# Delta rule stage of a two-layer kernel: joint level products, block-sized merges, a second state buffer, a transferred output matrix and new engine orders

## The reference

```python
q, k, v = short_conv(h @ Wq), short_conv(h @ Wk), short_conv(h @ Wv)    # 4 taps, then silu
g = exp(-softplus(h @ Wfa @ Wfb + dt_bias) * exp(A_log))                # per token, head, key
beta = sigmoid(h @ Wb);  q = l2norm(q) * DK ** -0.5;  k = l2norm(k)
def step(S, inp):                        # S: keys x values, one per head
    S = S * gt[..., None]
    pred = einsum('bhk,bhkv->bhv', kt, S)
    delta = (vt - pred) * bt[..., None]
    S = S + kt[..., None] * delta[:, :, None, :]
    o = einsum('bhk,bhkv->bhv', qt, S)
o = o * rsqrt(mean(o * o) + EPS) * norm_w * sigmoid(h @ Wga @ Wgb);  x = x + o @ Wo
```

## Time and profile before

| what | value |
|---|---|
| median of 3 runs | 1812.22 us (1808.32 to 1816.23) |
| the profiled execution's own time | 1804.4 us |
| its span, first to last instruction | 1802.4 us |
| busy in the span: TensorE, VectorE, ScalarE, GpSimd | 1547.0, 1338.2, 1034.1, 41.3 us |
| mean granted clock of TensorE | 0.93 |

### The profile page before, as it was taken

How to read it: one execution, slowest core, us unless ns; L and a number is a source line. 1 busy time by engine, 2 the same in 40 slices (tenths; PEclk the granted TensorE clock), 3 DMA queues, 4 the chain that set the end, 5 groups by cost and what they waited for, 6 DMA issues and landing times. The chain is left out here.

```text
span 1802.4 us, 33031 instructions
## 1 busy us (share of the span) xinstructions
PE 1547.0 (86%) x10840; PEld 1067.9 (59%) x10840; DVE 1338.2 (74%) x3718; ACT 1034.1 (57%) x2716; POOL 41.3 (2%) x49
## 2 busy tenths in 40 slices
PE   6867889786878778999999998999999899888678
PEld 2534555563535246767766766776777677677535
DVE  6649989956722388889889889888898998984121
ACT  6317878876310455866766676586676667643210
POOL 0000000000000000000000000000000000000000
PEclk9989899989889879999999999999999999989589
DMA  2023000001010211011201101111110110100010
GB/s 103 25 75 93 11 10 5 2 1 77 25 52 18 63 29 43 16 52 51 61 12 55 58 12 57 58 38 29 57 55 12 60 54 16 45 28 7 1 52 24
DMA packets 84071, 69.42 MB, mean 39 GB/s; under 512 B 58673, under 2 KB 72625, under 8 KB 82625
## 3 DMA queue, kind: packets, MB, share of 16 engines
q1 hardware_dynamic: 83904, 67.31, 12.3%
HBM read 58.33 MB, written 6.98 MB: 36 GB/s over the span
## 5 line engine op out<-in xcount | busy, mean ns | idle before, releaser
L1524 DVE SCALAR_TENSOR_TENSOR arena<-arena 128x1024 f32<-128x1024 f32 x144 | 184.1, 1279 | 30.6 <-ACT arena L1101 29.8
L789 PE MATMUL bank<-xt,arena 128*128 128x512 f32 x384 | 197.4, 648 | 4.5 <-ACT arena L1093 3.1
L1582 DVE COPY_PREDICATED arena<-arena,bank 128x512 f32<-128x512 int32 x160 | 185.0, 1175 | 0.3 <-issue 0.3
L842 PE MATMUL bank<-arena 128*64 128x64 f32 x3072 | 143.8, 238 | 36.6 <-DVE arena L1604 21.7
L842 PEld LDWEIGHTS bank<-arena 128*64 128x64 f32 x3072 | 117.0, 144 | 84.0 <-issue 54.6
L1602 DVE TENSOR_TENSOR arena<-arena 128x512 f32<-128x512 f32 x224 | 156.4, 698 | 3.3 <-PE bank L842 2.9
L639 PE MATMUL bank<-xt,arena 128*128 128x512 f32 x320 | 143.5, 604 | 5.5 <-DVE arena L1344 3.9
L789 PEld LDWEIGHTS bank<-xt,arena 128*128 128x128 f32 x384 | 73.7, 209 | 74.8 <-issue 71.8
L639 PEld LDWEIGHTS bank<-xt,arena 128*128 128x128 f32 x320 | 60.3, 193 | 89.6 <-issue 83.6
L658 PE MATMUL bank<-arena 128*128 128x256 f32 (+2 forms) x384 | 102.3, 416 | 11.0 <-DVE arena L1344 10.2
L1100 ACT COPY arena<-bank 128x512 f32<-128x512 f32 x96 | 56.5, 589 | 91.7 <-PE bank L789 91.7
(11 more groups left out here) (169 smaller groups left out, 3563.6 us busy)
## 6 DMA issues: line engine op xcount, KB each, us to landing
arena<-zero_scratch SPq DMA_DIRECT2D x29, 512.0 KB, 3.8
arena<-d_w SPq DMA_DIRECT2D x16, 519.0 KB, 6.1
arena<-beta_scratch SPq DMA_DIRECT2D x16, 512.0 KB, 5.4
arena<-f_up SPq DMA_DIRECT2D x2, 1408.0 KB, 6.3
arena<-w_scratch SPq DMA_DIRECT2D x2, 1376.0 KB, 6.1
arena<-f_idx SPq DMA_DIRECT2D x2, 1072.0 KB, 9.7
w_scratch<-arena SPq DMA_DIRECT2D x2, 1072.0 KB, 4.0
arena<-a_wq SPq DMA_DIRECT2D x16, 128.0 KB, 2.7
```

Source lines behind the costliest of these rows:

```text
L789: last = pe.matmul(bank[b][:], DW[:, par, c:c + P], XT[:, k, rhs], start=(k == 0), stop=(k == KC - 1))
L842: last = pe.matmul(to[:, :, p], KL[:, par, r], rhs, start=True, stop=True)
L1524: dve.scalar_tensor_tensor(out=CT[:, x], in0=RAW[:, x, 3 - j:3 - j + S], scalar=DW[:, par, tap:tap + 1], in1=CT[:, x], op0=ALU.mult, op1=A ...
L1582: dve.copy_predicated(out, mask, bank[b][:].rearrange("p (c b s) -> p c b s", c=8, s=s)).then_inc(free[b], 1)
```

## The change

Level products of both groups go into one bank (64 columns per chunk), banks 2 and 3 alternate by level, PE's step is split into `low` and `high` (`top` is level 6). The output matrix's lower half is therefore written at columns 0 to 63 and moved by a transfer (`mb_moved`), and the old place cleared (`mb_cleared`). Masks, XX and PM are 64 columns wide or less. `left` and `right` multiply diagonal blocks of 2s x 2s alone; at level 5 ACT copies instead of DVE. `norm_q` is four matmuls of 256 columns and a VectorE transpose. SS has two buffers, and `predict` and `update` lose their bank 6 matmuls to `out` and `out_end`. PLACE is new on all engines. Cut to its core:

```diff
+    "pe": [
+        (1.169, "piece", 3), (1.27, "piece", 2), (1.343, "piece", 6), (1.452, "piece", 7), (1.608, "piece", 5),
...
+        (2.56, "turn_v", 0), (2.586, "turn_v", 1), (2.6373, "low", 0), (2.6673, "high", 0), (2.6794, "low", 1),
+        (2.7104, "high", 1), (2.7247, "low", 2), (2.7502, "high", 2), (2.8123, "low", 3), (2.8214, "high", 3), (2.86, "norm_q"),
+        (2.9257, "low", 4), (3.0639, "high", 4), (3.123, "gate", 0), (3.2507, "low", 5), (3.285, "gate", 1),
+        (3.3144, "high", 5), (3.4294, "top", 1), (3.4295, "left", 4), (3.4541, "right", 4), (3.4915, "top", 0),
+        (3.5312, "left", 5), (3.5698, "right", 5), (3.6044, "left", 6), (3.6785, "right", 6), (3.699, "keys", 0),
+        (3.728, "solve", 0), (3.774, "update", 0), (3.7741, "out", 0), (3.814, "predict", 1), (3.883, "solve", 1),
+        (3.917, "update", 1), (3.9662, "out_end", 0), (3.991, "predict", 2), (4.0147, "out", 1), (4.025, "solve", 2),
...
+        (4.2582, "out_end", 4), (4.283, "solve", 5), (4.288, "out", 5), (4.295, "update", 5), (4.2955, "out_end", 5),
+        (4.32, "predict", 6), (4.337, "solve", 6), (4.3655, "out", 6), (4.367, "update", 6), (4.4079, "out_end", 6),
+        (4.426, "predict", 7), (4.452, "solve", 7), (4.4868, "out", 7), (4.4971, "out_end", 7), (4.552, "update", 7),
...
+        (5.322, "project", 1), (5.574, "project", 0),
...
+    "act": [
...
+        (3.264, "gate", 0), (3.328, "gate", 1), (3.3405, "level", 5), (3.4512, "left", 4), (3.4871, "top", 1),
...
+    "dve": [
...
+        (3.196, "less", 11), (3.212, "less", 12), (3.213, "less", 13), (3.224, "less", 14), (3.232, "advance", 4, 0),
+        (3.234, "total", 4), (3.252, "advance", 4, 1), (3.3037, "level", 4), (3.312, "total", 5), (3.356, "advance", 5, 0),
...
...
+                    sp.wait_ge(free[2], read(2, m, "low", LEVELS - 3))
+                    sp.wait_ge(free[3], read(3, m, "low", LEVELS - 2))
+                    sp.dma_start(MB[64:P, par, :, 1, 64:P], MB[64:P, par, :, 1, 0:64]).then_inc(mb_moved, 16)
                     sp.wait_ge(inverse_out, 32 * (m + 1))
                     wait(sp, x_zero, 16 * m)
                     wait(sp, y_zero, 16 * (m - 1))
                     for k in range(NB):
-                        ks = slice(BLK * k, BLK * (k + 1))
-                        sp.dma_start(XX[ks, :, ks], blk_x.rearrange("(k c) (i a) -> k i c a", k=NB, i=BLK)[k]).then_inc(x_put, 16)
+                        ks, at = slice(BLK * k, BLK * (k + 1)), BLK * k % 64
+                        sp.dma_start(XX[ks, :, at:at + BLK], blk_x.rearrange("(k c) (i a) -> k i c a", k=NB, i=BLK)[k]).then_inc(x_put, 16)
                         sp.dma_start(YY[ks, par, :, ks], blk_y.rearrange("(k c) (a i) -> k a c i", k=NB, a=BLK)[k]).then_inc(y_put, 16)
+
+                def clear(m, par):
+
+                    sp.wait_ge(mb_moved, 16 * (m + 1))
+                    sp.dma_start(MB[64:P, par, :, 1, 0:64],
+                                 zeros[64:P, 0:NT * 64].rearrange("p (c k) -> p c k", c=NT)).then_inc(mb_cleared, 16)
...
-                for t in range(NT):
-                    last = pe.matmul(bank[0][:, t:t + 1], RAW[:, 0, 4 + t * P:4 + (t + 1) * P], ONES[:, 0:1], start=True, stop=True)
+                q = RAW[:, 0, 4:].rearrange("p (c j i) -> p j c i", j=4, i=32)
+                for j in range(4):
+                    last = pe.matmul(bank[0][32 * j:32 * j + 32, 0:2 * P], ONES[:, 0:32], q[:, j], start=True, stop=True)
...
+            def dr_products(n, par, lv, gr):
+
+                b, s = 2 + lv % 2, 1 << lv
                 if lv == 0:
                     pe.wait_ge(key_step, done("dve", n, "key", 2))
                     pe.wait_ge(silu_ready, done("act", n, "silu", 0))
                 else:
                     pe.wait_ge(kq_step, done("dve", n, "advance", lv - 1, gr))
+                for c in range(4 * gr, 4 * gr + 4):
+                    for h in range(2):
+                        r = slice(c * P + 64 * h, c * P + 64 * h + 64)
+                        rhs = KQ[:, par, :, r].rearrange("p w (b r s) -> p w b r s", r=2, s=s)[:, :, :, 1, :]
+                        to = bank[b][64 * h:64 * h + 64, c * 64:(c + 1) * 64].rearrange("p (w b s) -> p w b s", w=2, s=s)
+                        last = pe.matmul(to, KL[:, par, r], rhs, start=True, stop=True)
+                return last
+
+            def dr_low(n, par, lv):
+
+                use(2 + lv % 2, n, "low", lv)
+                dr_products(n, par, lv, 0).then_inc(low_done, 1)
+
+            def dr_high(n, par, lv):
+
+                dr_products(n, par, lv, 1).then_inc(full[2 + lv % 2], 1)
...
+            def dr_left(n, par, lv):
+
+                b, w = 2 + lv % 2, 2 << lv
+                use(b, n, "left", lv)
                 if lv == BASE:
                     pe.wait_ge(x_put, 16 * NB * (n + 1))
-                    for high in range(BASE, LEVELS):
-                        pe.wait_ge(free[b], read(b, n, "level", high, gr))
                 else:
-                    pe.wait_ge(x_sel, done("dve", n, "right", lv - 1, gr))
-                for t in range(4):
-                    c = 4 * gr + t
-                    if lv < LEVELS - 1:
-                        last = pe.matmul(bank[b][:, t * P:(t + 1) * P], MB[:, par, c, 0, :], XX[:, c, :], start=True, stop=True)
-                    else:
-                        last = pe.matmul(bank[b][64:P, t * 64:(t + 1) * 64], MB[0:64, par, c, 0, 64:P], XX[0:64, c, 0:64],
+                    pe.wait_ge(free[4], read(4, n, "right", lv - 1))
+                if lv < LEVELS - 1:
+                    pe.wait_ge(free[b], read(b, n, "low", lv))
+                else:
+                    for gr in range(2):
+                        pe.wait_ge(free[2 + gr], read(2 + gr, n, "top", gr))
+                for c in range(NT):
+                    if lv == LEVELS - 1:
+                        last = pe.matmul(bank[b][64:P, c * 64:(c + 1) * 64], MB[0:64, par, c, 0, 64:P], XX[0:64, c, :],
                                          start=True, stop=True)
+                        continue
+                    for k in range(P // w):
+                        r, at = slice(k * w, (k + 1) * w), k * w % 64
+                        last = pe.matmul(bank[b][r, c * 64 + at:c * 64 + at + w], MB[r, par, c, 0, at:at + w],
+                                         XX[r, c, at:at + w], start=True, stop=True)
...
+                    to = bank[4][:, c * 64:(c + 1) * 64].rearrange("p (w b s) -> p w b s", w=2, s=s)
+                    for k in range(P // (2 * s)):
+                        r, at, b = slice(2 * s * k, 2 * s * (k + 1)), 2 * s * k % 64, 2 * s * k % 64 // (2 * s)
+                        pe.matmul(to[r, 0, b], YY[r, par, c, r], PM[r, c, at:at + s], start=True, stop=True)
+                    for k in range(P // (2 * s)):
+                        r, at, b = slice(2 * s * k, 2 * s * (k + 1)), 2 * s * k % 64, 2 * s * k % 64 // (2 * s)
+                        last = pe.matmul(to[r, 1, b], PM[r, c, at:at + 2 * s], YY[r, par, c, 2 * s * k + s:2 * s * (k + 1)],
+                                         start=True, stop=True)
...
-                use(6, n, "predict", c)
                 use(5, n, "predict", c)
                 pe.wait_ge(free[5], read(5, n, "update", c - 1))
                 pe.wait_ge(kq_step, done("dve", n, "advance", LEVELS - 1, c // 4))
-                pe.matmul(bank[5][:, 0:P], KQ[:, par, 0, c * P:(c + 1) * P], SS, start=True, stop=True).then_inc(full[5], 1)
-                pe.matmul(bank[6][:, 0:P], KQ[:, par, 1, c * P:(c + 1) * P], SS, start=True, stop=False)
+                pe.matmul(bank[5][:, 0:P], KQ[:, par, 0, c * P:(c + 1) * P], SS[:, c % 2, :], start=True,
+                          stop=True).then_inc(full[5], 1)
...
-                pe.matmul(bank[6][:, 0:P], MB[:, par, c, 1, :], DL[:, c % 2, :], start=(c == 0), stop=True).then_inc(full[6], 1)
+
+            def dr_out(n, par, c):
+
+                use(6, n, "out", c)
+                pe.wait_ge(free[5], read(5, n, "solve", c))
+                if c:
+                    pe.wait_ge(free[5], read(5, n, "update", c - 1))
+                    pe.matmul(bank[6][:, 0:P], KQ[:, par, 1, c * P:(c + 1) * P], SS[:, c % 2, :], start=True, stop=False)
+
+            def dr_out_end(n, par, c):
+
+                pe.wait_ge(mb_cleared, 16 * (n + 1))
+                pe.matmul(bank[6][:, 0:P], MB[:, par, c, 1, :], DL[:, c % 2, :], start=(c == 0),
+                          stop=True).then_inc(full[6], 1)
...
+            def dr_level(n, par, lv):
+
+                b = 2 + lv % 2
+                act.wait_ge(full[b], turn(b, n, "low", lv) + 1)
+                act.wait_ge(free[5 - b], read(5 - b, n, "low", lv - 1))
+                wait(act, full[6], read(6, n - 2, "out", NT - 1))
+                got = bank[b][:].rearrange("p (c w s) -> p c w s", c=NT, w=2)
+                for h in range(2):
+                    rows = slice(64 * h, 64 * h + 32)
```

(44 more changed lines are left out.)

272 lines of the change are left out of this document (115 added, 157 removed).

## The result

The changed kernel takes 1817.66 us (median of 19 runs, 1813.57 to 1827.50) against 1808.32 us (19 runs, 1803.90 to 1816.95): ratio 1.0047, 95% interval 1.0032 to 1.0063. It is slightly slower; the predicted 1786 us and its direction are wrong, the range 1735 to 1850 holds. Its profiled execution took 1823.99 us, span 1822.2 us.

What follows compares the result with a forecast made beforehand. No one engine bounds: TensorE is nearest, VectorE close, tripping over each other by 4.5 us per head. A net 1.7 us per head, times 15, is 26 us: 1804.4 to 1778 profiled, 1786 us median; range 1735 to 1850.

Steps and rivals of the forecast that it cites:

- the part on transfers: Move and clearing on SP: clearing hidden, but `left` 4's chain 1.1 us closer with 0.5 us more issue, 0.7 us wait per head.
- The rival on the other side: `left` 4 waits for the move: TensorE stands still 5.4 us per head, total 1847 us; chance 0.25.
- the sum: Per head: 3.2 us of waits returned, minus 0.8 TensorE work, minus 0.7 transfer wait, gives 1.7 us.
- VectorE's part: `level` merges 5.9 us less, `right` merges 2.4 less, transpose 0.3 more: 8.0 us less busy per head, 56.5 to 48.5.
- TensorE's part: Small blocks of `left`/`right` 1.2 us more, `norm_q` 0.8 less, tile entries 0.4 more: 0.8 us more work per head.
- The tiles rival: Diagonal tiles writing one bank do not overlap: 0.075 us per record, 1932 us, or some 1870 upward; chance 0.07.
- The waits behind VectorE: Of 3.5 us per head that TensorE waits for VectorE, 3.2 come back; bounds 1.5 and 4.5.
- The state chain: `predict` freed from bank 6, `update` writing the other state buffer: release counted within the 14.9 us of waits behind L1642.
- The ends of the stage: Last head's shorter merges 4 us less, a head's wider spread over the order 4 us more.
- The clock: Sign of a wrong forecast: granted clock in the steady part under 0.95, from standing still at `left` 4.

Runs made afterwards that it cites:

- experiment 1: The changed kernel with SyncE's output-matrix move and its two waits issued behind the inverse's sixteen transfers: 1702.8 us, ratio 0.9392 against the kernel before.
- experiment 6: On experiment 1, `out`/`out_end` right behind `predict`/`update`, with bank 6 wait: 1966.8 us; without that wait: 1924.1; only `turn_out` moved ahead: 1757.24.
- experiment 5: On experiment 1, work made twice: `left`/`right` block products (levels 4 and 5) 1858.56 us, level merges 1752.35 us, six wide products 1763.02 us.

## Why the prediction was wrong, point by point

- **The step that failed** is the last sentence of the part on transfers: "a wait of 0.7 us per head, which I count". It took the chain without the move's gate. Measured: 5.5 us of wait, 7.4 us of effect per head (experiment 1). The rival on the other side had worked the same wait out from the order tables as 5.4 us and named its point, level 5 read more than 3 us after the inversion's end; it was read 9.3 us after (1132.61 to 1141.88). That arithmetic used only lines that I had; the objection that offsets do not time the steps got a chance of 0.25 instead of 0.75. The sign went wrong there. That the time still fell into the stated range was luck: this wait and its effect, 7.4 us per head against the 0.7 in the sum, nearly cancelled a relief of TensorE that the sum did not have either.
- **VectorE's part** held: 8.0 us less forecast, 7.2 measured (56.5 to 49.3); the transpose takes 0.45 us where 0.3 was net added.
- **TensorE's part** was mis-sized, outside its bounds: the blocks 5.7 us where 11.8 was taken and 7.8 the low bound. The nearest row, L842, alternates between two tiles, the 32-wide blocks between four. `norm_q` takes 0.58 us for 8 records (from 1113.87 to 1114.45 in the changed kernel) where 0.9 was taken and 1.7 stood before. Together TensorE's work fell by some 6 us per head, where 0.8 more was forecast; over eight heads its busy time goes from 59.9 us (clock 0.98) to 52.8 in experiment 1 (clock 1.00), which is about 6 us at an equal clock. This is why the rival's mechanism ended at 1818 us and not at its 1847.
- **The tiles rival** is refuted: diagonal tiles that write one bank overlap, 0.034 us per record at `left` 5 where one tile of that size took 0.075. The rule of the Trainium skill ("TensorEngine Tiling (Array Packing)", Restrictions and Gotchas) that different row tiles can't write one bank at the same time does not hold here for tiles that differ in rows and columns.
- **The waits behind VectorE**: 3.2 of 3.5 us per head were to go. In the changed kernel L850, L936 and L947 (11.3 us) still wait 36 us in 12.5 heads, 2.9 us. Why they stay was not tested.
- **The state chain** was counted within the waits; experiment 6 shows that in the new order it carries far more, with the reserve named there.
- **The ends of the stage** were put at nothing net: the start costs 21 us, the end returns 7. In experiment 1 the start is at 716.0, so the wait is part of that too.
- **The clock** was listed as a sign of error and fell as said, 0.93, from standing still at `left` 4; its price, 2.6 us of slower work per head, was in no term.

## What to carry to other kernels

A wait put ahead of an in-order queue's issues delays everything behind it: before placing a transfer, ask what it waits for and who waits for what stands behind, and put the transfer that nobody needs soon last. Here that is one block of three lines and worth 6.5%. When a change relieves two engines that limit each other, relieve both and then look for the first wait that neither owns; TensorE's relief alone gave 1.1%, and VectorE's alone was not tried.

## What the runs showed of the hardware that was not expected

- A matmul and its weight load on 32 x 32 tiles follow the one before after 0.008 us (contraction 32, 16 columns) and 0.0106 us (32 columns) at a granted clock of 1.00, and after 0.016 us (32 columns) at 0.50, when neighbours lie on different diagonal tiles. On 64 x 64 tiles it is 0.034 us on two diagonal tiles in turn and 0.075 us on one.
- Long rows of such matmuls outrun instruction supply: pauses of up to 2.8 us, 128 pairs apart, in the rows of 256 records of experiment 5. The 128 records of `right` 4 shown above have none, but in experiment 1, at the full clock, pauses of up to 1.9 us come up at L915 and L918, 0.6 us per head on average.
- After a stand of 5 us TensorE's granted clock was 0.52 for 4.7 us, near the lower of its two levels (1.2 GHz): by that alone (4.7 x 0.48) the stand costs about 2.3 us more than itself, an estimate; measured over eight heads it was 2.6.
